# Attention with 16 mixed heads on one core: exponentials regrouped unscaled with their sums, the mixing weights scaled by the reciprocals on GpSimd

## The reference, cut to what matters

```
qkv  = layernorm(h) @ w_qkv                         # 16 heads of 64
attn = softmax(q k^T / 8)                           # [16 heads, 257 queries, 257 keys]
attn = einsum('bhij,hg->bgij', attn, reattn_w)      # the heads are mixed
attn = (attn - mean_g) * rsqrt(var_g + 1e-3) * gamma + beta
h    = h + (attn @ v) @ w_out + b_out
h    = h + ffn(layernorm(h))                        # gate, up, down
```

## Time and profile before

| | |
|---|---|
| Time of the program, median of 3 runs | 876.7 us (876.49 to 878.59) |
| The profiled execution's own time | 874.84 us |
| Its span, first to last instruction | 873.1 us |
| Granted TensorE clock, mean | 0.935 |
| TensorE busy (products / weight loads) | 732.1 us (84%) / 527.8 us (60%) |
| VectorE busy | 642.9 us (74%) |
| ScalarE busy | 435.2 us (50%) |
| GpSimd busy | 179.6 us (21%) |
| SyncE's DMA queue | 45.34 MB, 15.4% of 16 DMA engines |

### The profile page before, as it was taken

One profiled execution on the slowest core, in us unless ns is written; L12 is line 12 of the kernel. 1 busy time (PEld: TensorE's weight loads), 2 busy tenths in 40 slices (PEclk: granted clock), 3 DMA queues, 4 the chain that ended last, 5 costly groups with the idle time before them and its releaser, 6 DMA issues.

```text
span 873.1 us, 14228 instructions
## 1 busy us (share of the span) xinstructions
PE 732.1 (84%) x4514; PEld 527.8 (60%) x4514; DVE 642.9 (74%) x1442; ACT 435.2 (50%) x1198; POOL 179.6 (21%) x367
## 2 busy tenths in 40 slices
PE   1769688989998999898998999899998899788754
PEld 0446466757675777666775767477766677456521
DVE  1596758688958896888768885889688886868444
ACT  0103637563657364745747265836575574747210
POOL 0308124012310233013301231023301330013000
PEclk9959799989999999989998999899999999899877
DMA  8300410050003200230004000311023000500000
GB/s 330 129 1 0 172 46 2 17 175 9 31 1 129 72 30 0 85 107 12 24 28 164 6 30 0 128 64 36 0 73 119 13 1 28 166 7 7 1 12 0
DMA packets 25414, 49.26 MB, mean 56 GB/s; under 512 B 2715, under 2 KB 6052, under 8 KB 24740
## 3 DMA queue, kind: packets, MB, share of 16 engines
q1 hardware_dynamic: 24340, 45.34, 15.4%
q10 hardware_dynamic: 1040, 3.49, 1.0%
HBM read 13.16 MB, written 2.11 MB: 17 GB/s over the span
## 4 chain that ended last, share of the span: by engine, by line
PE 37%; issue 26%; DVE 16%; ACT 8%; POOL 8%; DMA 4%; POOLq 1%; SPq 0%; ACTq 0%; DVEq 0%
PE small L535 5%; PE big L535 5%; PE small L686 5%; PE big L552 5%; DMA pg<-pst 4%; PE big L618 4%; DVE pst L1186 3%; DVE mx L1193 2%; ACT pst L918 2%; PE big L716 2%; PE small L641 2%; PE small L671 2%; ACT ot L1007 2%; DVE var L1221 1%; POOL nww L1569 1%
## 5 line engine op out<-in xcount | busy, mean ns | idle before, releaser
L918 ACT ACTIVATE pst<-big,nb 128x256 f32<-128x256 f32 x256 | 117.7, 473 | 46.9 <-DVE nb L1196 24.5
L618 PEld LDWEIGHTS big<-w_mix,pg 128*128 128x128 f32 x1024 | 122.5, 194 | 25.9 <-DVE an L1265 18.3
L618 PE MATMUL big<-w_mix,pg 128*128 128x128 f32 x1024 | 126.3, 279 | 7.9 <-DVE an L1265 7.9
L1193 DVE TENSOR_REDUCE mx<-big 128x4 f32<-128x1024 f32 x64 | 78.2, 1222 | 26.2 <-PE big L552 25.7
L552 PE MATMUL big<-qk_t 64*128 64x256 f32 x512 | 72.6, 402 | 20.1 <-ACT qk_t L901 20.1
L939 ACT ACTIVATE sqb<-big 128x1024 f32<-128x1024 f32 x64 | 64.8, 1014 | 42.9 <-PE big L618 42.9
L1221 DVE TENSOR_REDUCE var<-sqb 128x64 f32<-128x1024 f32 x64 | 77.6, 1213 | 9.1 <-ACT sqb L939 9.1
L1265 DVE TENSOR_TENSOR an<-big,rstd 128x1024 f32<-128x1024 f32 x64 | 78.4, 1225 | 2.7 <-DVE rstd L1252 0.2
L1186 DVE TENSOR_SCALAR pst<-pst,rr 128x256 f32<-128x256 f32 x256 | 72.8, 350 | 0.0
L552 PEld LDWEIGHTS big<-qk_t 64*128 64x128 f32 x512 | 44.2, 186 | 45.6 <-ACT qk_t L901 27.9
L535 PE MATMUL small<-xnt,w_qkv 128*128 128x256 f32 x256 | 65.5, 400 | 0.0
(11 more groups left out here) (200 smaller groups left out, 1233.5 us busy)
## 6 DMA issues: line engine op xcount, KB each, us to landing
pg<-pst SPq DMA_DIRECT2D x128, 256.0 KB
w_qkv<-in_w_qkv SPq DMA_DIRECT2D x1, 3072.0 KB
xt<-in_x_t SPq DMA_DIRECT2D x8, 256.0 KB, 2.9
xr<-in_x_tok SPq DMA_DIRECT2D x8, 256.0 KB, 2.7
out<-h SPq DMA_DIRECT2D x16, 128.0 KB
an<-in_gate_t ACTq DMA_DIRECT2D x1, 1024.0 KB, 8.5
an<-in_up_t ACTq DMA_DIRECT2D x1, 1024.0 KB, 10.8
an<-in_down_t ACTq DMA_DIRECT2D x1, 1024.0 KB, 13.3
```

The costliest lines, as they stand in the source:

```text
L618: last = mm(mix_place(n)[:, i * P:(i + 1) * P], pg[:, hf * (IB // 2) + i, it * T + jt * P:it * T + (jt + 1) * P], w_mix[:], start=True, st ...
L918: last = A(pst[:, g % 2, h % GH, it, :], big[p % 2][:, (j * TT + it) * T:(j * TT + it + 1) * T], ACT.Exp, bias=nb[:, h, it:it + 1], scale= ...
L1193: V.reduce_max(mx[:, hs, :], big[p % 2][:, :].rearrange("p (h t l) -> p h t l", h=2, t=TT), AX)\
```

## The change

`normalise` is gone. The exponentials are regrouped as they are, and with each row go its two totals (one for each query half), which VectorE writes behind the row into `pst`: a row of the DMA is now 514 numbers, at a pitch of 520. `d`, `eck` and `tot` are made for each pair, and the DMAs of a pair wait for its `tot`. When all of an element's DMAs have landed, VectorE takes the reciprocals of the totals in `pg` (`row_scales`, 128x32), and GpSimd multiplies `w_mix` by them: 4096 weights per partition, one scaled 128x128 block for each query half and query set, in four instructions of 128x1024 (`scale_weights`). They lie in `pst`, which is free by then, and are what the mixing products multiply by. The product groups go by query half, then half of the query sets, then key half, so that two groups in a row use the same blocks.

```diff
@@ constants and tiles
+SUM = TT * T
+PW = SUM + QG
...
-    return n // 4, n // 2 % 2, n % 2
+    return n // 4, n % 2, n // 2 % 2
...
-        pst = sb("pst", [P, 2, GH, TT, T])
+        pst = sb("pst", [P, 2, GH, PW])
+        w_rows = pst[:].rearrange("p s j m -> p (s j m)")[:, 0:TT * IB * P].rearrange("p (t i x) -> p t i x", t=TT, i=IB)
...
-        pg = sb("pg", [P, IB, TT * T])
+        pg = sb("pg", [P, IB, PW])
+        rg = sb("rg", [P, TT, IB])
@@ sync: regroup
-                        if j % (GH // 2) == 0:
-                            sp.wait_ge(dve_s.sem, dve_s.at(b, (("p", j // (GH // 2)), g)))
                         h = g * GH + j
-                        sp.dma_start(pg[rows_of(h), :, :], pst[:, g % 2, j, :, :])\
+                        if j % 2 == 0:
+                            sp.wait_ge(dve_s.sem, dve_s.at(b, ("tot", h // 2)))
+                        sp.dma_start(pg[rows_of(h), :, 0:SUM + TT], pst[:, g % 2, j, 0:SUM + TT])\
                             .then_inc(s_sh[g % 2][j // 2], 16)
@@ tensor: mix_heads
+                if jt == 0:
+                    pe.wait_ge(pool_w.sem, pool_w.at(b, (it, hf)))
                 for i in range(IB // 2):
-                    last = mm(mix_place(n)[:, i * P:(i + 1) * P],
-                              pg[:, hf * (IB // 2) + i, it * T + jt * P:it * T + (jt + 1) * P], w_mix[:],
-                              start=True, stop=True)
+                    ib = hf * (IB // 2) + i
+                    last = mm(mix_place(n)[:, i * P:(i + 1) * P], pg[:, ib, it * T + jt * P:it * T + (jt + 1) * P],
+                              w_rows[:, it, ib, :], start=True, stop=True)
@@ scalar: scores
-                    if p % 2:
-                        act.wait_ge(dve_s.sem, dve_s.at(b, ("d", g)))
-                        hs = slice(g * GH, (g + 1) * GH)
-                        A(eck[:, hs, :], dck[:, hs, :], ACT.Exp).then_inc(act_s.sem, 1)
+                    act.wait_ge(dve_s.sem, dve_s.at(b, ("d", p)))
+                    hs = slice(2 * p, 2 * p + 2)
+                    A(eck[:, hs, :], dck[:, hs, :], ACT.Exp).then_inc(act_s.sem, 1)
@@ vector: scores
+                def total(p):
+                    hs = slice(2 * p, 2 * p + 2)
+                    dve.wait_ge(act_s.sem, act_s.at(b, ("eck", p)))
+                    V.tensor_tensor(pst[:, p // 2 % 2, 2 * (p % 2):2 * (p % 2) + 2, SUM:SUM + TT],
+                                    sums[:, hs, :], eck[:, hs, :], ALU.add).then_inc(dve_s.sem, 1)
...
-                def normalise(g, part):
-
-                    for j in range(part * GH // 2, (part + 1) * GH // 2):
-                        for it in range(TT):
-                            h = g * GH + j
-                            last = V.tensor_scalar(pst[:, g % 2, j, it, :], pst[:, g % 2, j, it, :],
-                                                   rr[:, h, it:it + 1], None, ALU.mult)
-                    last.then_inc(dve_s.sem, 1)
...
+            def row_scales(b):
+
+                for s in s_sh[0] + s_sh[1]:
+                    dve.wait_ge(s, 16 * 2 * (NGRP // 2) * (b + 1))
+                if not is_(b, 0):
+                    dve.wait_ge(pool_w.sem, pool_w.at(b - 1, (TT - 1, 1)))
+                V.reciprocal(rg[:], pg[:, :, SUM:SUM + TT].rearrange("p i t -> p t i")).then_inc(dve_w.sem, 1)
@@ vector: iteration
-                ffn_x(b, ff, P, 1, (dve_o.sem, dve_o.at(b, ("h3", 1))), lambda: ffn_out(b, ff, P, 0))
+                ffn_stats(b, ff, P, 1, (dve_o.sem, dve_o.at(b, ("h3", 1))))
+                if do_scores:
+                    row_scales(b + 1)
+                ffn_norm(b, ff, P, 1)
+                ffn_quant(b, ff, P, 1)
+                ffn_out(b, ff, P, 0)
@@ gpsimd
+            def scale_weights(b, it):
+                if it == 0:
+                    pool.wait_ge(dve_w.sem, dve_w.at(b, "rg"))
+                for hf in range(2):
+                    ibs = slice(hf * (IB // 2), (hf + 1) * (IB // 2))
+                    G.tensor_tensor(w_rows[:, it, ibs, :], w_mix[:].unsqueeze(1).to_broadcast([P, IB // 2, P]),
+                                    rg[:, it, ibs].unsqueeze(2).to_broadcast([P, IB // 2, P]), ALU.mult)\
+                        .then_inc(pool_w.sem, 1)
@@ gpsimd: iteration
                 power(b, ff["pool"], ff["dve"], ve_f, rs_f, P, slice(1, 2), ("ve", 1))
+                if do_scores:
+                    scale_weights(b + 1, 0)
                 if do_mixer:
                     mixer_out(b + 2)
+                if do_scores:
+                    scale_weights(b + 1, 1)
```

More of the change, by code:

```diff
@@ L179, in build @@
         eck = sb("eck", [P, H, TT])
-        tot = sb("tot", [P, H, TT])
         rr = sb("rr", [P, H, TT])
         pck = sb("pck", [P, TT, H])
-        pst = sb("pst", [P, 2, GH, TT, T])
+        pst = sb("pst", [P, 2, GH, PW])
+        w_rows = pst[:].rearrange("p s j m -> p (s j m)")[:, 0:TT * IB * P].rearrange("p (t i x) -> p t i x", t=TT, i=IB)
         sqc = sb("sqc", [H, T + 1])
@@ L305, in build @@
         act_s = stage("act_s", [("q", 0)] + [x for p in pairs for x in
-                      ([("q", p + 1)] if p < HP - 1 else []) + [("e", p)] + ([("eck", p // 2)] if p % 2 else [])
-                      ] + ["eq"])
-        finish = ["tot", "r", "pck", ("p", 0)]
+                      ([("q", p + 1)] if p < HP - 1 else []) + [("e", p), ("eck", p)]] + ["eq"])
+        finish = ["r", "pck"]
         dve_s = stage("dve_s", ["sck", "sq", "mq", "nq"]
                       + [x for p in pairs for x in
[L311 to L315, removed]
+                         [("mx", p), ("nb", p), ("d", p)] + ([("tot", p - 1)] if p else [])
+                         + ([(f, p // 2 - 1) for f in finish] if p and p % 2 == 0 else [])]
+                      + [("tot", HP - 1)] + [(f, NGRP - 1) for f in finish] + ["rq", "pq", "pckt"])
         pool_s = stage("pool_s", ["pcc"])
+        dve_w = stage("dve_w", ["rg"])
+        pool_w = stage("pool_w", [(it, hf) for it in range(TT) for hf in range(2)])
         r_order, sq_order, a_order = [], [("sq", 0), ("ln", 0), ("ex", 0), "qs", "cs", ("sq", 1)], [("v", 0)]
@@ L917, in scores @@
                             h = 2 * p + j
-                            last = A(pst[:, g % 2, h % GH, it, :],
+                            last = A(pst[:, g % 2, h % GH, it * T:(it + 1) * T],
                                      big[p % 2][:, (j * TT + it) * T:(j * TT + it + 1) * T], ACT.Exp,
@@ L1166, in scores @@
                     first()
+                def total(p):
[3 more added lines that the diff above has]
+                                    sums[:, hs, :], eck[:, hs, :], ALU.add).then_inc(dve_s.sem, 1)
                 def finish_group(g):
                     hs = slice(g * GH, (g + 1) * GH)
[L1170 to L1173, removed]
+                    dve.wait_ge(dve_s.sem, dve_s.at(b, ("tot", 2 * g + 1)))
+                    V.reciprocal(rr[:, hs, :], pst[:, g % 2, :, SUM:SUM + TT]).then_inc(dve_s.sem, 1)
                     dve.wait_ge(dve_s.sem, dve_s.at(b, ("r", g)))
@@ L1178, in finish_group @@
                                     ALU.mult).then_inc(dve_s.sem, 1)
-                    normalise(g, 0)
-                def normalise(g, part):
-                    for j in range(part * GH // 2, (part + 1) * GH // 2):
-                        for it in range(TT):
-                            h = g * GH + j
-                            last = V.tensor_scalar(pst[:, g % 2, j, it, :], pst[:, g % 2, j, it, :],
-                                                   rr[:, h, it:it + 1], None, ALU.mult)
-                    last.then_inc(dve_s.sem, 1)
                 for p in pairs:
@@ L1197, in scores @@
                                            op0=ALU.mult, op1=ALU.min).then_inc(dve_s.sem, 1)
-                    if p % 2:
-                        g = slice(p // 2 * GH, (p // 2 + 1) * GH)
-                        dve.wait_ge(dve_s.sem, dve_s.at(b, ("nb", p)))
-                        V.tensor_tensor(dck[:, g, :], nb[:, g, :], nsck[:, g, :], ALU.subtract)\
-                            .then_inc(dve_s.sem, 1)
-                        if p > 2:
-                            normalise(p // 2 - 1, 1)
-                    elif p:
+                    dve.wait_ge(dve_s.sem, dve_s.at(b, ("nb", p)))
+                    V.tensor_tensor(dck[:, hs, :], nb[:, hs, :], nsck[:, hs, :], ALU.subtract)\
+                        .then_inc(dve_s.sem, 1)
+                    if p:
+                        total(p - 1)
+                    if p and p % 2 == 0:
                         finish_group(p // 2 - 1)
@@ L1208, in scores @@
                         between[p]()
+                total(HP - 1)
                 finish_group(NGRP - 1)
-                normalise(NGRP - 1, 1)
                 dve.wait_ge(act_s.sem, act_s.at(b, "eq"))
@@ L1492, in _ @@
             mixer_y(1)
+            row_scales(0)
             mixer_out(1)
@@ L1651, in _ @@
             mixer_values(1)
+            scale_weights(0, 0)
             mixer_out(1)
```

(1 more changed line is left out.)

## The result

The changed kernel takes **920.7 us** (median of 4 runs, 919.42 to 920.97) against 876.6 us (4 runs, 876.35 to 878.59): ratio 1.0495, 95% interval 1.0477 to 1.0513. It is slower, by 44 us. The profiled execution took 920.91 us, its span 919.1, at a mean granted clock of 0.901, 0.935 before.

A forecast was written before the change was run, and what follows sets the result against it. TensorE was taken as busiest, VectorE work counting only where TensorE waits. Per batch -1.1 + 2.5 + 3.8 + 0.85 + 0.8 = +6.85, six times, plus 1.4 and 1.8: +44.3 on 874.84, 919.1; median 921 us, range 892 to 944.

The forecast's parts named there:

- Scores, -1.1 a batch: End of the scores: regrouping DMAs start earlier per pair, ScalarE's waits for them go, gaining 1.1 us a batch, bounds 0 to 3.3.
- First pair, +2.5: Second feed-forward tile: GpSimd's first two scalings hold VectorE's normalising and quantising, costing 2.5 us a batch, bounds 2.4 and 4.3.
- Newton's step +3.8: Ahead of mixing product 3: the other two scalings delay GpSimd's Newton step, costing 3.8 us a batch, bounds 3.4 and 4.7.
- gate +0.85: Second tile's gate product: the longer TensorE pause before it lowers the clock in every batch, costing 0.85 us.
- The clock behind product 3, +0.8 with bounds 0 to 1.7: Mixing: a pause grown to some 4 us ahead of product 3 slows the first products behind it, 0.8 us a batch.
- Start +1.8: Beginning of the run: a wait of 1.72 us goes, but Newton's first step comes 3.8 later, together 1.8 us.
- Seventh iteration, -1.1 + 2.5 = +1.4: Seventh iteration: no `h` work on GpSimd, so scalings end before Newton's step; only scores' gain and second-tile hold remain, 1.4 us.
- Nothing for the order, `row_scales`, the small exponentials: Key-half mixing order, VectorE's reciprocals of totals, and eight small `eck`, `d`, `tot` steps were each to cost nothing.
- the milder case: Rival, chance 0.17: clock kept in the scores, GpSimd at lower bounds, second pause costing no clock; slower, but only 892 us.
- "VectorE is not held": Faster rival, chance 0.06: second-tile normalising and quantising run unheld beside GpSimd's first two scalings, 1.4 us less a batch, 867 us.
- "regrouping becomes the bound": Rival, chance 0.04: longer rows double each regrouping transfer to 3.2 us, about 21 us more a batch, 1020 us.

The follow-up runs named there:

- the unscaled kernel with the memsets: The changed kernel without GpSimd's scaling, softmax division left out, with 46 memsets ahead of VectorE's first instruction to move its loop code: 856.3 us, ratio 0.9801.
- the last version: The changed kernel with scalings spread over GpSimd's iteration, 46 memsets in front, and waits ahead of the fourth and, in the seventh iteration, third scaling: 859.4 us, ratio 0.9790.
- the unscaled kernel: The changed kernel with no scaling on GpSimd, mixing products taking unscaled weights, softmax division left out: 871.2 us, ratio 0.9958.
- the first pair alone: The changed kernel with only the first two of four scalings kept, plus 46 memsets in front of VectorE's first instruction: 879.0 us, ratio 1.0011.

## Why the prediction was right, and where it was not

The forecast was 921 us, the result 920.7. The direction and the two main costs were right for the reasons given: the hold on VectorE's quantising chain, and Newton's step queued behind the scalings. That the numbers lie 0.3 us apart is luck. The sum gave 919.1 for the profiled execution and that took 920.9; the 1.9 us added on top, because the median of the kernel before lay that much above its profiled execution, happened to make up for it (here the median lies 0.2 below). And within a period a term that was too small by 1.1 us stands against the other three, which came out lower than I had them by 0.2, 0.3 and 0.2. Point by point:

- *Scores, -1.1 a batch.* Measured -1.28. The DMA waits went, the first transfer went 7.6 us behind A where I had 7.8, ScalarE's copies became the bound, and the pause in front of pair 7's products is 1.16 us. That the clock might stay up was kept as a bound (3.3); in the unscaled kernel with the memsets A to B is 39.57 us, 2.0 under before, and 0.75 under the changed kernel, which runs the same code there.
- *First pair, +2.5.* Measured +2.16, confirmed by adding a wait (the 2.16 came back) and by halving the instructions. I had the pair take 4.05 us (394.65 to 398.7); it took 3.79, and the last quantising step came behind it as foreseen.
- *Newton's step +3.8, gate +0.85.* Together measured +4.42, C to D. In the third iteration, where it is 4.55, GpSimd's work on `h` starts 7.31 us behind the turn and not 6.35: VectorE waited for ScalarE's tanh behind the slow gate product (1.29 us, 0.33 before). So some 0.95 is the gate, 3.6 Newton's step.
- *The clock behind product 3, +0.8 with bounds 0 to 1.7.* **This is the term that was mis-sized.** D to A grew by 1.94 us in the mean and by 2.6 (31.55 to 34.15) in four of the six iterations, over the upper bound. I had allowed the low clock for product 3 alone or half of it; it stayed for product 3 (3.78 for 2.05) and for the down product (1.91 for 1.04). Where the pause was only 1.04 us (before, and the last version) product 3 took 2.05 in nearly every iteration.
- *Start +1.8.* A of iteration 1 came 2.0 us later (158.74, then 160.73).
- *Seventh iteration, -1.1 + 2.5 = +1.4.* It cost 2.3 us up to D, of which 1.7 came back behind D (from A to the program's last instruction 148.07 us before, 148.72 after). But its parts were others. I had the four scalings end before Newton's step and so cost nothing more; they ran without a break beside the whole quantising chain, and B to C grew by 3.8 us (8.66 to 12.47), TensorE waiting 5.41. The scores gained 2.5. Its timelines of GpSimd and VectorE:

```profile
810.70 7.59 POOL L1616 TENSOR_TENSOR pst<-w_mix,rg 128x1024 f32<-128x1024 f32 x4
...
813.61 1.02 DVE L1314 TENSOR_SCALAR xn<-xn,sx 128x256 f32<-128x256 f32 x1
814.67 1.87 DVE L1317 TENSOR_SCALAR xq<-xn 128x256 bf16<-128x256 f32 x1
816.46 1.84 DVE L1319 TENSOR_TENSOR cg<-am,w_mean 128x1 f32<-128x1 f32 x1
```

- *Nothing for the order, `row_scales`, the small exponentials.* The order: shown. The others: covered by the unscaled kernel being faster, not tried one by one.
- *What the sum did not have:* VectorE's loop code moved and was fetched anew at each jump back. Here that cost nothing, only because Newton's step was late by as much. That 921 came out so close owes something to this.

Of the rivals, the milder case fell because the clock did not stay up at the end of the scores (0.50 from 389.50 to 391.50 us) and the second pause did cost clock; "VectorE is not held" fell with the four rows of 1.98, 2.19, 2.18 and 0.93 us; "regrouping becomes the bound" with a stream of 26 us.

What stays open: why the low clock reaches further in one kernel than in another. Behind the same pause of 3.01 us ahead of the turn, the stretch from the gate product to the token projection (`w_qkv`) took 8.5 us with the first pair alone (399.33 to 407.85) and 9.3 in the changed kernel (414.85 to 424.13), against 7.25 before. Open too is why 1.7 us came back behind the seventh iteration's D.

## What to carry to other kernels

Work moved to GpSimd is paid for by VectorE: before placing it, list which VectorE instructions run beside it, and keep it clear of those with two SBUF inputs, however small (the 128x1 `cg` took 1.84 us for 0.15), and of `tensor_scalar`s from SBUF to SBUF. Among the latter a 128x2 one was held too, by the scaling that the added wait had moved:

```profile
408.82 1.75 DVE L1102 TENSOR_SCALAR ve_a<-mv_a 128x2 f32<-128x2 f32 x1
```

(0.17 us otherwise.) Those of one number a row were not held: 0.15 to 0.21 us beside a scaling in the changed kernel, as elsewhere. A wait in front of the GpSimd instruction can be the faster program. If a variant pauses at the loop's end with no releaser and its instruction queue moves more than before, move the code before drawing conclusions from its time. And take away suspected costs in pairs: two that end together can hide each other.

## What the runs showed that I had not expected

- A loop whose code moved by 46 instructions on one engine changed the time by 15 us (871.2 to 856.3), with 20 packets and 0.16 MB less of instruction traffic.
- An added wait won 18 us.
- A 128x64 `scalar_tensor_tensor` was held from 0.22 to 1.90 us, and that with the low clock behind it cost 3.3 us a batch (95.5 against 92.2).
- The `tensor_tensor` of 128x1024 with two repeated operands took 1.90 us in the mean on GpSimd in the last version, as the prediction had continued it from the smaller ones, and 1.99 in the changed kernel, where VectorE's held instructions go in between.
